# Three attentions with heads of 8 in one kernel: score products in 64 rows, two heads side by side

## The reference

```python
# rms: q and k divided by their root mean square
scores = q @ k.T                        # 16 heads, 512 x 512, contraction over 8
# decay: causal, with a second product of 6-vectors ("lines")
logits = q @ k.T * 8 ** -0.5 + (read_lines @ J_write.T) * decay ** (tq - tk) * scale
# relative: a bias by bucketed distance
scores = q @ k.T + rel_emb[bucket(tk - tq)]
out = softmax(scores) @ v @ W_out
```

## Time and profile before

| | us |
|---|---|
| median of three runs | 6195.84 |
| the profiled execution, its own time | 6193.98 |
| its span in the profile | 6191.6 |
| TensorE busy | 5058.1 (82%) |
| VectorE busy | 3678.4 (59%) |
| ScalarE busy | 3310.3 (53%) |
| GpSimd busy | 1366.9 (22%) |
| mean granted TensorE clock | 0.904 of full |
| DMA over the span | 46 GB/s |

### The profile page before, as it was taken

The page is one execution under the profiler, slowest core; times in us unless marked ns, Lnnn a source line. Parts: engine busy times, 40 slices in busy tenths (PEclk is TensorE's granted clock), DMA queues, the critical chain, the costliest instruction groups (busy, mean ns, idle before and its releaser), DMA issues. The chain is left out here.

```text
span 6191.6 us, 95542 instructions
## 1 busy us (share of the span) xinstructions
PE 5058.1 (82%) x30276; PEld 2635.5 (43%) x30276; DVE 3678.4 (59%) x7598; ACT 3310.3 (53%) x5224; POOL 1366.9 (22%) x1260
## 2 busy tenths in 40 slices
PE   6999859488888859868888838699999999999657
PEld 2333459444444449722222335333433334334435
DVE  4333465577677775466666674276676665765662
ACT  5888625345555514456666503466666665665212
POOL 1000127424334216611111028200000000000147
PEclk9999869799999959989999858899999999999768
DMA  3323222322232221232222213200000000000213
GB/s 94 83 69 75 64 44 50 78 65 81 79 91 79 83 50 44 67 82 62 60 60 61 66 34 56 54 1 0 0 0 0 0 0 0 0 0 0 64 26 50
DMA packets 239102, 290.13 MB, mean 47 GB/s; under 512 B 35542, under 2 KB 192950, under 8 KB 238756
## 3 DMA queue, kind: packets, MB, share of 16 engines
q1 hardware_dynamic: 204604, 245.06, 15.3%
q0 software_dynamic: 34176, 40.86, 3.7%
HBM read 189.22 MB, written 96.17 MB: 46 GB/s over the span
## 5 line engine op out<-in xcount | busy, mean ns | idle before, releaser
L995 ACT ACTIVATE prob_relative<-slot_relative 128x1024 f32<-128x1024 f32 x512 | 499.8, 1041 | 140.9 <-PE obank_relative L861 139.1
L2708 ACT ACTIVATE prob_wide<-slot_wide 128x1024 f32<-128x1024 f32 x512 | 494.0, 1016 | 149.7 <-PE slot_wide L2607 149.7
L1326 DVE TENSOR_TENSOR slot_decay<-slot_decay,dtab_decay 128x512 f32<-128x512 f32 (+3 forms) x1024 | 454.0, 494 | 191.3 <-PE slot_decay L821 172.2
L995 ACT ACTIVATE prob_decay<-slot_decay 128x640 f32<-128x640 f32 x512 | 358.8, 706 | 387.0 <-PE slot_decay L842 386.3
L995 ACT ACTIVATE prob_rms<-slot_rms 128x1024 f32<-128x1024 f32 x512 | 497.8, 1038 | 74.1 <-PE slot_rms L836 72.2
L2607 PE MATMUL slot_wide<-qT_wide,kT_wide 64*128 64x512 f32 x2048 | 508.8, 615 | 2.9 <-ACT prob_wide L2708 2.9
L1338 DVE TENSOR_TENSOR prob_relative<-prob_relative,rtab_relative 128x512 f32<-128x512 f32 (+1 forms) x512 | 410.0, 850 | 127.2 <-ACT prob_relative L995 116.7
L2620 PE MATMUL obank_wide<-prob_wide,v_wide 128*64 128x512 f32 x2048 | 467.7, 598 | 1.8 <-DVE zT_wide L2770 1.8
L2073 POOL TENSOR_TENSOR xn_choice_b<-X,stats_choice_b 128x512 f32<-128x512 f32 x8 | 8.4, 1047 | 1893.2 <-DVEq L2255 1893.2
L861 PE MATMUL obank_relative<-prob_relative,vaug_relative 128*32 128x512 f32 x2048 | 291.9, 644 | 116.9 <-DVE prob_relative L1338 115.3
L2756 DVE TENSOR_TENSOR sums_wide<-sums_wide,prob_wide 128x1024 f32<-128x1024 f32 x256 | 313.6, 1225 | 28.7 <-ACT prob_wide L2708 0.2
(11 more groups left out here) (838 smaller groups left out, 10618.8 us busy)
## 6 DMA issues: line engine op xcount, KB each, us to landing
scratch_decay<-parts_decay SPq DMA_DIRECT2D x192, 128.0 KB, 2.4
qst_rms<-scratch_rms SPq DMA_DIRECT2D x64, 288.0 KB
kst_rms<-scratch_rms SPq DMA_DIRECT2D x192, 96.0 KB
qst_relative<-scratch_relative SPq DMA_DIRECT2D x64, 288.0 KB
kst_relative<-scratch_relative SPq DMA_DIRECT2D x192, 96.0 KB
qst_decay<-scratch_decay SPq DMA_DIRECT2D x128, 128.0 KB
scratch_rms<-parts_rms SPq DMA_DIRECT2D x96, 128.0 KB, 2.3
kst_decay<-scratch_decay SPq DMA_DIRECT2D x192, 64.0 KB
```

The source lines that it names most:

```text
L995: nc.scalar.activation(prob[:, Q % 2, j, 0:c1 - c0], slot[:, u % 3, c0:c1], ACT.Exp).then_inc(exp_done, 1)
L1326: last = nc.vector.tensor_tensor(sl, sl, dtab[:, h, 0:m], ALU.mult)
L2708: nc.scalar.activation(prob[:, Q % 2, u % 4, :], slot[:, u % 2, :], ACT.Exp).then_inc(exp_done, 1)
```

## The change

The stacks of rms and relative hold six products of parts as decay's do (48 rows of 8; the products mid x low, low x mid and low x low are left out), and every stack fits in 64 rows. Two heads that are four apart share a stack position, one in rows 0 to 63 and one in rows 64 to 127; `head` gives the order. The stacks are half as long, and decay gets a stack `lst` for the query side of its lines. A unit is now one key block of two heads: its two matmuls contract over 64 rows each, in different rows, and write the two banks of the slot. In decay a unit thus has two times 512, 128, 384 or 256 columns. The exp, the decay multiply (now one instruction) and the band multiply (one for four heads and one key block) follow. The stacks are renewed in two halves of eight heads: a half is 12 DMAs in rms and relative and 22 in decay, and its first S waits for all of them. The second half's renewal waits for the last S of the batch. The mask product in decay stays 128x128.

```diff
-        NP = 6 if decay else 9
-        STACKED = 16 * (11 if decay else 5)
+        STACKED = 16 * 2 * (11 if decay else 6)
-        SR = NP * DH
-        KR = 2 * SR if decay else SR + 12 if relative else SR
+        HR = P // 2
+        SR = 6 * DH
+        KR = SR + 12 if relative else SR
...
-        qst = sb("qst", [P, H, S], BF16)
-        kst = sb("kst", [P, H, S], BF16)
-        kin = sb("kin", [P, H, S], BF16) if decay else None
+        qst = sb("qst", [P, H // 2, S], BF16)
+        kst = sb("kst", [P, H // 2, S], BF16)
+        lst = sb("lst", [P, H // 2, S], BF16) if decay else None
+        kin = sb("kin", [P, H // 2, S], BF16) if decay else None
...
-        stacked = [sem(f"stacked{g}") for g in range(NG)]
+        stacked = [sem(f"stacked{f}") for f in range(2)]
...
+        def half_rows(k, r0=0, r1=HR):
+            return slice(HR * k + r0, HR * k + r1)
+
+        def head(g, j):
+            return G * (g - g % 2) + 2 * (g % 2) + j % 2 + G * (j // 2)
...
         def unit(u):
-            Q, j = u // 4, u % 4
-            return G * (Q // 2) + j, Q // 2, Q % 2, j
+            Q, p = u // 4, u % 2
+            return Q // 2, blocks(Q % 2)[u % 4 // 2], p, 2 * (Q // 2) + p
...
         def span(kb):
             if decay:
-                return P * kb, (0, P, S, S)[kb], S - P * kb
+                return P * kb, (0, 0, S - P, S)[kb], S - P * kb
             return 0, kb % 2 * S, S
...
-                def stack(g, l, side):
...
+                def stack(f, l, side):
+                    to = slice(G * f, G * f + G)
+                    st = ((qst, kst), (lst, kin))[l][side]
+                    for k in range(2):
+                        heads = slice(2 * G * f + G * k, 2 * G * f + G * k + G)
+                        if side == 0:
+                            src = scr[2 * l, 0:2 * DH, heads, :].unsqueeze(1).to_broadcast([2 * DH, 2, G, S])
+                            sp.dma_start(st[half_rows(k, 0, 4 * DH), to, :], src).then_inc(stacked[f], 16)
+                        else:
+                            src = scr[2 * l + 1, :, heads, :].rearrange("(d j) h t -> d j h t", j=3)[:, 1:3]
+                            for x in range(2):
+                                sp.dma_start(st[half_rows(k, 2 * DH * x, 2 * DH * (x + 1)), to, :], src
+                                             ).then_inc(stacked[f], 16)
                         src = by_part[2 * l + side][0:3:2, :, heads, :].rearrange("a d h t -> d a h t")
+                        sp.dma_start(st[half_rows(k, 4 * DH, 6 * DH), to, :], src).then_inc(stacked[f], 16)
+                        if l == 0 and side == 0:
+                            sp.dma_start(st[half_rows(k, KR, KS), to, :], no_shift).then_inc(stacked[f], 16)
...
-                            values["used", g] = b * UNITS + 8 * (g + 1)
+                            values["used", f] = b * UNITS + UNITS // 2 * (f + 1)
...
-                            for g in range(2 if l < NL - 1 else NG):
-                                for k in range(0 if g >= 2 else l, l + 1):
+                            for f in range(1 if l < NL - 1 else 2):
+                                for m in range(0 if f else l, l + 1):
...
                     if step == "S":
...
-                            if kp == 0 and j == 0:
-                                pe.wait_ge(stacked[g], (b + 1) * STACKED)
+                            if u % (UNITS // 2) == 0:
+                                pe.wait_ge(stacked[g // 2], (b + 1) * STACKED)
                             slot_free(pe, b, u)
-                        for kb in blocks(kp):
-                            q0, at, m = span(kb)
+                        q0, at, m = span(kb)
+                        for k in range(2):
                             last = nc.tensor.matmul(
-                                slot[:, u % 3, at:at + m], kst[:, h, kb * P:(kb + 1) * P],
-                                qst[:, h, q0:S], start=not decay, stop=not decay, skip_group_check=True)
+                                slot[:, u % 3, k * S:k * S + m], kst[half_rows(k), pair, kb * P:(kb + 1) * P],
+                                qst[half_rows(k), pair, q0:S], start=not decay, stop=not decay, skip_group_check=True)
                         if decay:
-                            for kb in blocks(kp):
-                                q0, at, m = span(kb)
-                                last = nc.tensor.matmul(slot[:, u % 3, at:at + P], identb[:], negb[:],
+                            for k in range(2):
+                                last = nc.tensor.matmul(slot[:, u % 3, k * S:k * S + P], identb[:], negb[:],
                                                         start=False, stop=True, skip_group_check=True)
...
-                        nc.scalar.activation(prob[:, Q % 2, j, 0:c1 - c0], slot[:, u % 3, c0:c1],
+                        nc.scalar.activation(prob[:, Q % 2, p:G:2, at:at + m],
+                                             slot[:, u % 3].rearrange("p (k c) -> p k c", k=2)[:, :, 0:m],
                                              ACT.Exp).then_inc(exp_done, 1)
...
                     if step == "I":
...
-                            sl = slot[:, u % 3, at:at + m]
-                            last = nc.vector.tensor_tensor(sl, sl, dtab[:, h, 0:m], ALU.mult)
+                        sl = slot[:, u % 3].rearrange("p (k c) -> p k c", k=2)[:, :, 0:m]
+                        nc.vector.tensor_tensor(sl, sl, dtab[:, head(g, p):head(g, p) + G + 1:G, 0:m], ALU.mult
+                                                ).then_inc(biased, 1)
...
                     if step == "BAND":
...
-                            last = nc.vector.tensor_tensor(v, v, rtab[:, h:h + 2, c0:c0 + (hi - lo) * P], ALU.mult)
+                        kb = blocks(kp)[half]
...
+                        last = nc.vector.tensor_tensor(v, v, of_group(rtab, g)[:, :, :, c0:c0 + (hi - lo) * P], ALU.mult)
```

130 lines of the change are left out of this document (55 added, 75 removed).

## The result

The changed kernel takes 6239.62 us (median of 4 runs, 6238.03 to 6242.66) against 6195.49 for the kernel before in the same comparison: a ratio of 1.0072, 95% interval 1.0059 to 1.0084. It is 44 us slower where 79 us less were forecast. The profiled execution has a span of 6237.5 us, 45.9 more than before.

A forecast was written before the change was run, and what follows sets the result against it. Rms was taken as held by TensorE with ScalarE close behind, decay by TensorE plus a hole at the batch's start, relative by a ring of waits. Rms -45, relative -46, decay +5, starts +7: 6193.98 - 79 = 6115 us, range 6015 to 6200.

The forecast's parts named there:

- rival 2: Score products: bf16 pairs do not overlap, so nothing is saved and the switches remain; 6410 us, chance 0.06.
- the switch: TensorE, all three stages: each change of tile mode costs 0.10 us, with 0.19 as upper end.
- The new wait for the stacks: Rms, each batch's first S: stacks come 2.2 us late, ScalarE bridges 1.0, leaving about 1.2 us per batch.
- today 2.5 us go lost on top of the fuller engine: Rms: the same loss on top of ScalarE's 35.2 us gives 37.8 to 38 a batch, 39.2 with the stacks' wait.
- TensorE's +0.6 a batch: Decay: columns save 8.5 us, mask switches add 6.4 and other switches 2.7, net +0.6 us per batch.
- VectorE's relief: Decay: one multiply per unit instead of two, up to 7 us less per batch, of which 0.3 was counted.
- the size of the units: Decay: units of 1024 to 256 columns instead of even 640 lengthen some waits, shorten others; bounds -1.5 and +3 us.
- Starts: Stage beginnings: rms +3 us for more stack orders, relative +4 for the second bias load; +7 in all.
- of the 4.8 us that TensorE gains I let 2.9 reach the ring: Relative: the loop of exp, band multiply and PV shortens by 2.9 us per batch, 46 us in all.
- rival 1: Decay: switches at 0.19 to 0.20 us cost more than halves save; 6290 us, deciding from about 0.14; chance 0.13.
- Rival 4: Clock: it falls where TensorE idles; relative at 0.85 would take +64 us, 6180 in all; chance 0.10.
- Rival 3: Rms and relative: stacks land in time and TensorE's saving counts whole, 162 us less; 6045 us, chance 0.18.

The follow-up runs named there:

- e6: e2 with one pair of products issued twice per unit (S in rms and relative, I in decay), same result: 6241.0 us, ratio 1.0075.
- e14: e9 with rms's stacks put back where the change has them, not earlier: 6271.5 us, ratio 0.9909 to the kernel before.
- e9: e5 with rms's stacks earlier and rms's weighted sums (PV) one unit later: 6245.0 us on another chip, ratio 0.9851 to the kernel before.
- e12: Kernel before with only rms's weighted sums and the copy of their result one unit later: 6301.6 us, ratio 0.9963.
- e8: Kernel before with only decay's mask product in 64-row form, adding two tile-mode switches in each unit that had none: 6243.6 us, ratio 1.0081.
- e2: Changed kernel with decay's mask product in 64-row form, no switches between S, mask and I, guard pass in pairs: 6178.8 us, ratio 0.9971.
- e5: e2 with decay's units reordered so that a large and a small one alternate: 6169.3 us, ratio 0.9953.
- e13: Changed kernel, its switches kept, with decay's units in e5's alternating order: 6355.6 us on another chip, ratio 1.0035 to the kernel before.
- e11: e5 with ten unread products on TensorE ahead of decay's guard wait at each batch's start: 6349.7 us on another chip, ratio 1.0025.

## Why the prediction was wrong

**Right.** The pair costs 0.21 and overlaps wholly (rival 2 false), the switch 0.11 us against 0.10 taken, so TensorE's work in rms and relative fell nearly as worked out. Worked out were 16 x 5.1 = 82 and 16 x 4.8 = 77 us; busy time fell by 50 and 48, with more of it at the half clock. With the time that TensorE was busy at half speed counted half, the trace gives 69 and 72. The new wait for the stacks came where it was put, 2.2 us a batch against the computed 2.2; its orders, in SP's queue of the changed kernel, and the S that waits:

```profile
341.29 1.38 SPq L618 DMA_DIRECT2D kst_rms<-scratch_rms  x2
...
344.80 0.65 SPq L621 DMA_DIRECT2D kst_rms<-scratch_rms  x1
```

```profile
347.89 1.04 PE L841 MATMUL slot_rms<-qst_rms,kst_rms 64*128 64x512 bf16 x4 [2.50 <-DMA kst_rms<-scratch_rms]
```

The last order is issued at 345.45 and S runs 2.4 later, the 2.3 taken for landing. The rule of the Trainium skill (TensorEngine Tiling (Array Packing), Key Properties) that a change of tiling mode drains TensorE holds here, at 0.11 us a time. The prediction also set the Trainium skill's 3.07 times for four tiles of 32 rows (TensorE: Matmul & The Clock Gate, Measured speedup) beside its own term. No run here has such tiles; two tiles of 64 gave 2.0 times, so the 0.28 a pair estimated by that efficiency did not come.

**Rms, 46 us off: the step "today 2.5 us go lost on top of the fuller engine; on top of 35.2 that gives 37.8 to 38".** I took the loss as a constant above the fuller engine. It is no such thing. S of a unit is queued behind the PV of older units, which waits for ScalarE, and ScalarE then waits for that S; a faster TensorE waits longer at the PV (27.9 to 53.0 us). Of 5.1 us net, 1.7 reached the exps outside the border (e6 says much the same there, 2.7 for 7.0), and the wait for the stacks took 1.8 back, for which I had counted 1.2. The runs price both: the late stacks at 1.7 a batch (e14 against e9, with PV late), and PV in S's way at half of what pairs are worth, 0.9 against 1.8. That e9 measures the forecast's 39.2 is chance. The forecast had 1.2 us of wait in it, which e9 hasn't, and 1.4 of e9's 3.2 are due to the later PV alone, which the kernel before can have without pairs (e12). Without the wait I gave pairs 4.0 a batch, and at best they brought 1.8. What takes the rest isn't shown; the one large wait of TensorE left in e9 is for a slot that ScalarE has to free (21.6 us).

**Decay, 41 us off: the step that set TensorE's +0.6 a batch, VectorE's relief against it, and called the size of the units a bound.** Three terms were missed. (1) The switches: I netted 9.1 us of them against 8.5 us of columns, as if both were worth the same. In e8 and e2 the unit's own two switches have the largest price of the three: e8 puts 5.0 us of work a batch into the old kernel's units (switches, less the shorter mask product), and 2.5 show; e2 takes 8 out of the changed one's, and 2.1 show. That they count because they stand in the ring multiply, S, mask, exp, slot free, is how I read it and was not run apart. Of the columns little shows: with these switches gone and the order of (2) mended, e5's batch is 0.8 below the kernel before for 8.5 us of columns less, with 27 other switches and a lower clock against it. Whether a microsecond of columns is worth less than one of switches the runs leave open. (2) Units of 1024, 1024, 256, 256 columns in a row cost 1.1 to 1.2 a batch (e5, e13); I had them at "some longer and others shorter" between -1.5 and +3. (3) The clock: at e11's rate of 1.5 us for 6.4, decay's 80 us more at half speed (5.0 a batch) are at most 1.2 a batch, 19 us in all; this one is worked out, not run, and part of it may be in (1) and (2) already. The three come to 2.5 + 1.2 + 1.2 = 4.9, and the batch grew by 2.5 (57.9 to 60.4), so the columns gave back at most some 2.4 of 8.5, as an estimate.

**Starts, 15 off: a term that was not there.** I listed memsets, fills and orders, and passed over the guard pass at decay's first batch, though the diff touches it. The section on the change says that this pass only takes the new indices; its products also went from 96 rows to 64. There each product of 512 columns stands between two masks of another mode, so that nothing pairs. The timeline of the pass before:

```profile
1248.15 0.38 PE L770 MATMUL slot_decay<-kst_decay,qst_decay 96*128 96x512 bf16 x1
1248.37 0.22 PE L775 MATMUL slot_decay<-identb_decay,negb_decay 128*128 128x128 bf16 x1
1248.43 0.38 PE L770 MATMUL slot_decay<-kst_decay,qst_decay 96*128 96x512 bf16 x1
```

One product and mask took 0.28, then 0.76 (1246.24 to 1247.00 above): 0.54 for the same work at half speed, 0.22 for two switches. 64 of them are 48.6 us where the pass took 24.6; 23.1 show. For relative's start I had +4, in TensorE's wait for the second bias rows. That wait is 13.5 us in place of 13.9, so the term was nothing. The start came 4.6 earlier in all, 3.1 of that before relative's first instruction of TensorE; why, no run shows. Rms's start was right (+2.9 for +3).

**Relative, 23 off: "of the 4.8 us that TensorE gains I let 2.9 reach the ring".** Sign and mechanism stood, the size was half: 1.45 a batch. e6 puts the exchange at 0.2, and the clock, 0.96 to 0.92, is in that number. I read it as the ring's wait for VectorE's band multiply, which only changed from two instructions to one; no run takes relative's ring apart, so the cause of the shortfall stays open between the two.

**The rivals.** The slower side was rival 1's, which the range left out, but not by its price: the switch is 0.11, not 0.19, and below the 0.14 that I gave as the turning point. The turning point itself was wrong, since it was worked out from gains in rms and relative that were not there. Rival 4, the clock, is real in all three stages: its mean fell from 0.99 to 0.97, 0.95 to 0.91 and 0.96 to 0.92. That an idle TensorE falls to 1.2 GHz is what the Trainium skill says (TensorE: Matmul & The Clock Gate, The HAM clock gate), and the fall behind rms's wait for the stacks, shown below, agrees. Its price is an estimate in decay (at most 19 us), is contained in relative's shortfall, and was not run apart in rms, where a stretch of 3.4 us at half speed follows each wait for the stacks. Rival 3 counted 162 us for rms and relative; e9, with the stacks in time and PV out of the way, has 71.

## What to carry to other kernels

Time saved on an engine counts only at the rate at which the kernel answers to it, and that can be measured before anything is built: issue one of its products twice (e6 did it on a later kernel, and got 0.2 us for one in two stages and 0.4 in the third), and look in the list of waits for what is queued ahead of the work that was made faster. When work goes into another tile mode, keep everything between two uses of it in that mode, the small mask products too, and look at every place where the products stand, the passes that run once included. Where units become unlike, do not let large ones follow each other.
